# A mixture-of-experts convolution with nine extra matmuls a turn, two parts of taps, later picks and an earlier exponent

## The reference

```python
feat = patched.mean(axis=(2, 3))
logits = feat @ Wg + bg
probs = jax.nn.softmax(logits, axis=-1)
routing = jax.nn.one_hot(jnp.argmax(logits, axis=-1), E, dtype=probs.dtype) * probs
...
y = jax.lax.conv_general_dilated(patched, w_, (1, 1), 'SAME', dimension_numbers=('NCHW', 'OIHW', 'NCHW'))
return jax.nn.relu(y + b_[None, :, None, None])
...
combined = jnp.einsum('ne,encij->ncij', routing, outs)
```

## Time and profile before

| | us |
|---|---|
| median of 3 runs | 192.06 |
| lowest and highest | 191.08, 193.27 |
| profiled execution, time | 194.34 |
| profiled execution, span of the core | 192.5 |
| TensorE busy in it | 107.7 |
| VectorE busy | 120.5 |
| ScalarE busy | 90.2 |
| GpSimd busy | 75.1 |

### The profile page before, as it was taken

One profiled execution on the slowest core, in us unless ns is written; L12 is line 12 of the kernel. 1 busy time (PEld: TensorE's weight loads), 2 busy tenths in 40 slices (PEclk: granted clock), 3 DMA queues, 4 the chain that ended last, 5 costly groups with the idle time before them and its releaser, 6 DMA issues.

```text
span 192.5 us, 11462 instructions
## 1 busy us (share of the span) xinstructions
PE 107.7 (56%) x4894; PEld 103.0 (54%) x4894; DVE 120.5 (63%) x271; ACT 90.2 (47%) x252; POOL 75.1 (39%) x236
## 2 busy tenths in 40 slices
PE   0003180495396703974199708990599356949940
PEld 0003080495396603964199608990599255939940
DVE  4699961292199338980899168942999166284274
ACT  2594136856572257346572549352745622650000
POOL 0760348074503463045613435343605563556000
PEclk9999998559969975699756985596559969995896
DMA  5974996366779898999989998998899698898602
GB/s 180 505 301 189 235 368 240 134 234 145 244 185 416 200 340 238 334 322 248 315 263 386 175 386 223 413 199 336 227 372 298 252 222 324 235 279 261 249 0 109
DMA packets 40545, 50.93 MB, mean 265 GB/s; under 512 B 31024, under 2 KB 33200, under 8 KB 39472
## 3 DMA queue, kind: packets, MB, share of 16 engines
q1 hardware_dynamic: 36880, 37.73, 63.7%
q10 hardware_dynamic: 3648, 13.02, 17.6%
HBM read 17.32 MB, written 14.43 MB: 165 GB/s over the span
## 4 chain that ended last, share of the span: by engine, by line
DMA 33%; PE 25%; SPq 20%; DVE 9%; issue 5%; ACTq 4%; ACT 2%; DVEq 0%
PE conv_bank L523 21%; DMA XG<-windows 19%; SPq L175 15%; DMA XG<-XG 12%; SPq L145 5%; PE pick_bank L511 3%; DMA XT<-x 3%; ACT WS L442 2%; ACTq L125 2%; ACTq L135 2%; DVE STATS L266 1%; DVE BLK L338 1%; DVE WP L361 1%; DVE ROWSUM L282 1%; DVE BLK L342 1%
## 5 line engine op out<-in xcount | busy, mean ns | idle before, releaser
L523 PE MATMUL conv_bank<-XG,WS 128*32 128x64 f32 x4800 | 94.7, 252 | 47.3 <-DMA XG<-XG 43.2
L523 PEld LDWEIGHTS conv_bank<-XG,WS 128*32 128x32 f32 x4800 | 90.2, 131 | 49.4 <-DMA XG<-XG 44.7
L223 POOL COPY WS<-WP 128x192 f32 x200 | 61.5, 355 | 94.9 <-issue 63.4
L442 ACT COPY WS<-WP 128x192 f32 x200 | 54.7, 348 | 66.3 <-issue 38.7
L331 DVE STREAM_TRANSPOSE YT<-conv_bank 128x320 f32<-128x320 f32 x40 | 19.6, 502 | 16.5 <-PE conv_bank L523 16.5
L266 DVE BATCH_NORM_STATS2 STATS<-XT 128x6 f32<-128x512 f32 x16 | 10.2, 680 | 26.4 <-DMA XT<-x 26.4
L338 DVE STREAM_TRANSPOSE BLK<-YT 128x1024 f32<-128x1024 f32 x8 | 17.9, 2242 | 1.1
L505 PE MATMUL logit_bank<-GATE,CONST 128*100 128x8 f32 x40 | 5.8, 253 | 20.7 <-DVE GATE L296 20.7
L434 ACT COPY WIND<-XN 128x2500 f32<-128x2500 f32 x7 | 16.6, 2375 | 0.2
L505 PEld LDWEIGHTS logit_bank<-GATE,CONST 128*100 128x100 f32 x40 | 4.9, 188 | 21.7 <-issue 15.6
L511 PE MATMUL pick_bank<-PROB,CONST 100*128 100x1 f32 x36 | 8.4, 338 | 9.3 <-DVE PROB L314 9.3
(11 more groups left out here) (37 smaller groups left out, 49.1 us busy)
## 6 DMA issues: line engine op xcount, KB each, us to landing
XG<-XG SPq DMA_DIRECT2D x30, 490.0 KB, 3.9
windows<-WIND ACTq DMA_DIRECT2D x8, 1250.0 KB
XG<-windows SPq DMA_DIRECT2D x60, 125.0 KB, 3.4
XT<-x SPq DMA_DIRECT2D x8, 512.0 KB, 6.1
XG<-XG SPq DMA_DIRECT2D x16, 240.0 KB
out<-XT SPq DMA_DIRECT2D x7, 512.0 KB, 6.0
XG<-windows SPq DMA_DIRECT2D x32, 62.5 KB, 2.7
XG<-ones ACTq DMA_DIRECT2D x1, 1250.0 KB, 11.2
```

The source lines that it names most:

```text
L223: last = nc.gpsimd.tensor_copy(WS[:, at % RING, ACT_PAIRS + i, :], WP[:, bass.ds(index[i], PAIR)])
L442: last = nc.scalar.copy(WS[:, at % RING, i, :], WP[:, bass.ds(index[i], PAIR)])
L523: last = nc.tensor.matmul(o, WS[:, lot, n % LOT * 2 + b // 2, column:column + C], taps, start=kx == 0, stop=kx == TAPS - 1)
```

## The change

Five edits come together. `warm()` issues nine matmuls of 512 columns (32 columns of `CONST` as weights, 512 as moving data) into a bank `warm_bank` that nothing reads, behind each group's logits. `PART` has two parts, lots 0 and 1 and lots 2 to 4, so there are four reads and two shifts fewer in a turn. The store of group g-1 stands on SyncE behind the second part's reads, no longer ahead of the first part's shifts. The picks stand behind lot 1. At the start, ScalarE takes the exponent of group 1 and then `root(2)` behind the copies of lot 1, and VectorE's `routing(1)`, `probability(1)` and `deviation(2)` stand ahead of the loop.

```diff
-PART = (0, 2, 4, LOTS)
+PART = (0, 2, LOTS)
...
+WARM = 9
...
-            read_upper(0, 2)
             shift(sp, 0, 1)
-            shift(sp, 0, 2)
...
-                if g > 0:
-                    store(g - 1)
                 if g + 1 < GROUPS:
                     shift(sp, g + 1, 0)
                     read_upper(g + 1, 1)
-                    read_upper(g + 1, 2)
+                if g > 0:
+                    store(g - 1)
+                if g + 1 < GROUPS:
                     shift(sp, g + 1, 1)
-                    shift(sp, g + 1, 2)
...
             statistics(2)
+            routing(1)
+            probability(1)
+            deviation(2)
 
             for g in range(GROUPS):
-                if g + 1 < GROUPS:
+                if 0 < g and g + 1 < GROUPS:
                     routing(g + 1)
-                if g + 2 < GROUPS:
+                if 0 < g and g + 2 < GROUPS:
                     deviation(g + 2)
-                if g + 1 < GROUPS:
+                if 0 < g and g + 1 < GROUPS:
                     probability(g + 1)
-                else:
+                if g + 1 == GROUPS:
...
-            for lot in range(1, LOTS - 1):
-                copies(0, lot)
+            copies(0, 1)
+            exponent(1)
             root(2)
+            copies(0, 2)
+            copies(0, 3)
             for g in range(GROUPS):
                 copies(g, LOTS - 1)
-                if g + 1 < GROUPS:
+                if 0 < g and g + 1 < GROUPS:
                     exponent(g + 1)
...
+            def warm():
+                for _ in range(WARM):
+                    nc.tensor.matmul(warm_bank[0:C, :], CONST[:, 0:C], CONST[:, 0:HALF], start=True, stop=True)
...
-                    if lot == 0:
+                    if lot == 1:
                         pe.wait_ge(pick_ready, turn)
                         pe.wait_ge(own_ready, turn)
                         picks()
                     if lot == LOTS - 1:
                         pe.wait_ge(gate_ready, turn)
                         logits()
+                        warm()
```

More of the change, by code:

```diff
@@ L93, in build @@
         conv_bank = [bank(f"conv_bank{i}") for i in range(NCB)]
-        logit_bank, pick_bank = bank("logit_bank"), bank("pick_bank")
+        logit_bank, pick_bank, warm_bank = bank("logit_bank"), bank("pick_bank"), bank("warm_bank")
         windows_dram = [nc.dram_tensor(f"windows{u}", (GI * C * NP, WIN * WIN), fp32).ap() for u in range(WB)]
@@ L201, in _ @@
                     load_x(g + 3)
+                if g + 1 < GROUPS:
+                    shift(sp, g + 1, 0)
+                    read_upper(g + 1, 1)
                 if g > 0:
@@ L204, in _ @@
                 if g + 1 < GROUPS:
-                    shift(sp, g + 1, 0)
-                    read_upper(g + 1, 1)
-                    read_upper(g + 1, 2)
                     shift(sp, g + 1, 1)
-                    shift(sp, g + 1, 2)
             for q in range(2):
```

## The result

The changed kernel takes 203.3 us (median of 4 runs, 199.27 to 206.53), the kernel before 192.67 us in the same sitting; the ratio is 1.044 with a 95% interval of 1.023 to 1.065. The profiled execution took 204.76 us with a span of 202.9; it is one of the two longer of the four, so its turns are read beside those of the experiments.

What follows compares the result with a forecast made beforehand. It took a chain of waits with a nearly full DMA queue as the bound. 51.5 + 20.3 + 3 x 19.5 + 2 x 18.5 + 10.3 + 8.2 gave 185.8 us, applied to the median 185 us, range 177 to 193.

Steps and rivals of the forecast that it cites:

- The lengths of the block: Nine 512-column matmuls behind each group's logits: 0.86 us each at full clock, 7.7 us together, at most 8.4.
- rival C: All goes well (turns of 18.5 us, 178.5 us) or the block takes about 4.7 us (178 us); chance 0.13.
- The turn: One loop pass per group: 18.5 us by lot 2's late shifts, 19.4 us of queue work, so 19.5 us per full turn.
- 7.5 to 9 us behind S0: Landing of the whole second part (lots 2 to 4), counted from the first part's shifts; 7.5 us used in the sum.
- the sum of 185.8: Start, full turns, turns 5 and 6, last lots and last block added up: 185.8 us against a span of 192.5.
- The store: The 512 KB store behind the second part's reads: worth 0 to 1.3 us of the chain, nothing with a full queue.
- The start: Time until group 1's lot 0 begins: 51.5 us instead of 52.96, bounds 49.5 and 53.5.
- I keep half of them: Two waits of 2 us each inside group 0's lots, half kept: those lots end at 43.3 us instead of 41.3.
- Picks and exponent: Picks leave the chain, gain inside lots 0 and 1's 3.5 us; early exponent sends group 1's first reads near 32.4, not 41.03.
- The queue's bound: DMA queue in full turns: 19.4 us of work, so a shorter chain can win about one us per full turn.
- Rival D: The block outlasts TensorE's hole and delays lot 0 and the queue; slower from a 9.2 us block, 199 us at 10; chance 0.12.

Runs made afterwards that it cites:

- e4: The kernel before with two parts of taps alone, its store ahead of the first part's shifts: 207.7 us.
- e7: The changed kernel with its two parts cut behind lot 2 (lots 0 to 2, lots 3 and 4), block kept: 193.8 us, ratio 1.002.
- e1: The changed kernel with the block of nine matmuls left out: 210.2 us, ratio 1.088.
- e5: The kernel before with the picks behind lot 1 and the early exponent alone (three parts, no block, store where it was): 185.1 us, ratio 0.961.
- e6: e5 with the store moved behind the last reads (the changed kernel with three parts and no block): 193.9 us, ratio 0.999.
- e13: The kernel before with the picks behind lot 1 alone, the exponent where it was: 188.1 us.
- e12: e5 with a block of five matmuls added: 189.9 us, ratio 0.988.
- e9: e5 with a block of nine matmuls added: 194.0 us, ratio 1.000.

## Why the prediction was wrong

**The lengths of the block: right.** 0.86 us for a matmul of 512 columns at full clock, 7.7 us for nine, were forecast; 7.76 was measured. The Trainium skill's figure of 216 ns for 512 columns ("TensorE: Matmul & The Clock Gate", Back-to-back issue gap), with the four passes for fp32 of its "FP8 and Floating Point Precision" (TensorE Precision Notes), gives an estimate of 7.8 us, and the trace agrees; its 131 ns for a long stream, and with it rival C's short block, doesn't hold here.

**The turn: wrong, and the main error.** The step was "With lot 2 late: S0 lands at ... 16 us after the turn's start and S1 7.5 us later, at 23.5". It tied S1 to S0 by a distance taken from the kernel before, and took 7.5 us although the row beside it says 11.6 for the last lot. S0 landed where it was forecast, some 16 us into the turn, but S1 landed 12 to 15 us behind it (landings worked out from the issues and their times to landing in four turns). There is a second tie, which that kernel's three parts kept slack: the reads of a part may begin only when the convolution has finished the same lots of the group before, since `XG` has one copy. With lots 2 to 4 as one part this is lots 2 to 4, reads, landing, shifts, landing, lots 2 to 4. Its terms measured 5.3 us at full clock (up to 7.9 where the lots begin at half), 5.8 from the first read's issue to the shift's, and 9.2 to the landing; whole cycles took from 20.7 us (132.75 to 153.42) to 22.9, against the 19.5 forecast. e4 (two parts alone, 11 to 15 us slower) and e7 (the cut moved by one lot, 8 to 9.5 us faster) show it. The "7.5 to 9 us behind S0" of the part-by-part sum was a range for a landing that isn't a property of the part, but of when its reads may begin and of what meets it in the queue. Of the 17.1 us between the sum of 185.8 and the span of 202.9, 8.9 lie in the start, 7.1 in the six turns and 1.1 behind them; the turn is the main error all the same, since in e1 a start 11 us earlier brought lots 2 to 4 only 1.3 us forward.

**The store: wrong in sign.** "Worth 0 to 1.3 us of the chain ... and nothing once the queue is full" had no loss in it. e5 and e6, which differ in it alone, are 8.8 us apart (7 by the ratios): the issue and the transfer stand ahead of S1, and the pushed S1 meets the write on ScalarE's queue. The prediction never placed ScalarE's write in the turn at all.

**The start: wrong by 9 us.** "43.3, logits 43.8, block 51.5 us" became 50.5 for the end of the lots and 61.3 for the end of the block. Two terms failed. "I keep half of them", of the waits of two us in group 0's lots: they aren't waits of a fixed length. The first pass stops at the same few records whatever the kernel, and the last piece was resumed at 47.6 to 50.9 us, whether TensorE had reached it 1 or 5.8 us earlier (52.4 in e13). And the block there ran at half clock for its first 4 to 5 us (10.0 us for 7.7), because the stops had let the clock fall ahead of it; the prediction priced it at full clock everywhere. The shifts for lots 2 to 4 also landed at 38.8 instead of 36 us.

**Picks and exponent: right, and underrated.** R0 of group 1 went out at 33 us (forecast 32.4), and the picks' us left the chain. Alone the two give 8 us (e5). The sum counted 1.5 us of the start for the exponent, since the block behind it "eats the rest", and hid the picks' gain in the lots' clock.

**The queue's bound: right, and read too weakly.** e5 has full turns of 19.2 to 19.6 us with cold lots, and in no kernel here do the second to fourth turns average below that. The prediction said that the queue leaves about one us per full turn to be won, and still gave TensorE a block to win it. The picks win it for nothing.

**Rival D: the right side with the wrong point.** It asked for a block of 9.2 us before the kernel becomes slower. On e5's base a matmul of the block costs 0.8 to 1.0 us on the mean, with five as with nine (e12, e9), because the queue-bound turns have no use for the clock. D was priced as if the other edits' gains in the same sum were secure.

## What to carry to other kernels

With one buffer that is refilled by parts, each part has a cycle of its own: use, refill, landing, use. Write down the sum for every part, and not only for the one that is late today; joining two parts adds their use and their bytes to one cycle. A transfer that is moved in a queue is paid by whatever stands behind it, and its price depends on what another queue sends at that moment; place the other queue's transfers in the turn before the sum is made. Work that only keeps the clock up is worth something only where TensorE's own pace is in the cycle that sets the turn: look first at whether the turn is at the queue's bound.

## What the runs showed of the hardware that had not been expected

TensorE's first pass through the loop's body stops behind 206, 326 or 327, 454 and 581 convolution records, not behind each of them in every kernel, for 0.2 to 5.8 us, with "issue" as the releaser; later passes don't. Packets of 0.02 MB on the instruction queues stand near some of the stops (in the kernel before between 36 and 40, 44 and 46, and 48 and 50 us, with stops that end at 46.98 and 50.91), so fetched code is a likely cause, but no run took it away, and it was only argued. The block behind such a stop began at half clock in the changed kernel and in e9 (granted clock 0.50 from 50 to 54 us).

The clock fell after a shorter rest than in the earlier trace rows. In the changed kernel, behind the picks, which end at 83.6 us:

```profile
85.00:86.00 1.00, 0.00 (x0) 0.00 (x0) 1.00 (x4) 0.03 (x1) 0.00 (x0) 1.00 0.97 399
86.00:87.00 1.00, 0.00 (x0) 0.00 (x0) 1.00 (x1) 1.00 (x5) 0.65 (x3) 0.80 1.21 353
87.00:88.00 1.00, 0.09 (x4) 0.10 (x8) 0.93 (x4) 0.34 (x2) 0.86 (x3) 0.50 0.67 164
```

The grant fell some 3 us behind the last matmul, and lots 2 to 4 of that group took 7.8 us. In the turns at 125 and 146 us it held through waits of 2.9 and 3.1 us, and yet in the turn at 103 us it fell within a wait of 2.7 us, some 2.4 us behind the picks, which end at 108.1:

```profile
109.00:110.00 1.00, 0.00 (x0) 0.00 (x0) 1.00 (x4) 0.00 (x0) 0.00 (x0) 1.00 0.90 274
110.00:111.00 1.00, 0.16 (x8) 0.16 (x12) 1.00 (x2) 0.98 (x4) 0.92 (x4) 0.75 1.02 251
111.00:112.00 1.00, 1.00 (x44) 1.00 (x44) 0.96 (x3) 0.73 (x4) 0.74 (x4) 0.50 0.92 172
```

So the length of the wait alone does not tell whether the clock falls.

Four shifts, two of 490 and two of 240 KB, land in 3.2 us each (the median) when they are issued ahead of the write of 1.25 MB from the other queue, and in 7.1 us when they are issued into it behind a store of 512 KB (e5 and e6).
